# Softmax denominators of a graph attention layer: from matmuls in the aggregation to running sums over the sorted edges in the projection

## The reference

```python
xp = (x @ W).reshape(N, H, C)
e = leaky_relu(a_src[src] + a_dst[dst], 0.2)      # edges and one loop per node
m = segment_max(e, dst)
ee = exp(e - m[dst])
z = segment_sum(ee, dst)                          # the denominators
alpha = ee / z[dst]
out = segment_sum(xp[src] * alpha[:, :, None], dst)
x = x + relu(out + bias)
```

## Time and profile before

| what | value |
|---|---|
| median of the three runs | 1515.13 us (1513.52 to 1517.62) |
| profiled execution | 1526.42 us, span 1524.7 us |
| projection begins, by the first weights of line 1555 on the timeline | about 140 us |
| aggregation, from the end of the projection | about 519 to 1212 us |
| finish | about 1212 to 1524.7 us |

### The profile page before, as it was taken

One profiled execution on the slowest core, in us unless ns is written; L12 is line 12 of the kernel. 1 busy time (PEld: TensorE's weight loads), 2 busy tenths in 40 slices (PEclk: granted clock), 3 DMA queues, 4 the chain that ended last, 5 costly groups with the idle time before them and its releaser, 6 DMA issues. The chain is left out here.

```text
span 1524.7 us, 29568 instructions
## 1 busy us (share of the span) xinstructions
PE 1327.2 (87%) x10150; PEld 902.0 (59%) x10150; DVE 1081.6 (71%) x2255; ACT 1006.7 (66%) x2253; POOL 672.7 (44%) x610
## 2 busy tenths in 40 slices
PE   7998577899997678889899988888998769999997
PEld 5775244554443367777677777776777634544543
DVE  7997489889833567666676666676676787777771
ACT  3667478885445467777777777776777665666652
POOL 1003411111255466666666566665666244443441
PEclk9999799999998899999999999999999979999999
DMA  6784475543463698988898998988888857767752
GB/s 233 275 297 134 138 251 184 181 157 119 152 215 111 235 317 313 317 310 299 305 309 307 309 349 303 316 301 292 306 309 300 306 162 189 195 173 195 188 141 48
DMA packets 110549, 363.62 MB, mean 238 GB/s; under 512 B 20204, under 2 KB 20988, under 8 KB 110148
## 3 DMA queue, kind: packets, MB, share of 16 engines
q0 software_dynamic: 66048, 225.15, 45.7%
q1 hardware_dynamic: 40996, 135.71, 26.0%
q10 hardware_dynamic: 3360, 0.91, 0.2%
HBM read 299.78 MB, written 72.85 MB: 244 GB/s over the span
## 5 line engine op out<-in xcount | busy, mean ns | idle before, releaser
L1783 PE MATMUL sum_ps<-xg,wgt 128*128 128x256 f16 x4992 | 602.5, 277 | 91.5 <-issue 66.8
L1757 ACT ACTIVATE wgt<-hot,tables 128x128 f16<-128x128 f16 x1664 | 503.0, 388 | 187.8 <-PE sum_ps L1783 61.5
L1783 PEld LDWEIGHTS sum_ps<-xg,wgt 128*128 128x128 f16 x4992 | 475.5, 99 | 185.3 <-issue 112.8
L1682 POOL DMA_INDIRECT xg<-d_xp,tables x404 | 414.1, 1025 | 243.9 <-issue 98.3
L1555 PE MATMUL xp_ps<-acc 128*128 128x512 f16 x1152 | 274.3, 387 | 21.7 <-issue 11.9
L1741 DVE TENSOR_TENSOR acc<-sum_ps,acc 128x1024 f32 x220 | 268.1, 1219 | 1.4 <-issue 1.3
L2180 PE MATMUL fmm_ps<-xg,tables 128*128 128x512 f16 x1200 | 265.0, 381 | 4.0 <-DVE tables L2009 4.0
L2180 PEld LDWEIGHTS fmm_ps<-xg,tables 128*128 128x128 f16 x1200 | 117.8, 98 | 141.8 <-issue 7.1
L1555 PEld LDWEIGHTS xp_ps<-acc 128*128 128x128 f16 x1152 | 108.9, 99 | 146.6 <-issue 28.5
L1740 DVE TENSOR_TENSOR zsum<-z_ps,zsum 128x8 f32 x220 | 35.5, 162 | 217.1 <-PE z_ps L1793 75.4
L1712 DVE TENSOR_TENSOR wgt<-hot,tables 128x512 f16<-128x512 f16 x416 | 157.8, 418 | 0.0
(11 more groups left out here) (320 smaller groups left out, 1526.4 us busy)
## 6 DMA issues: line engine op xcount, KB each, us to landing
d_xnT<-acc SPq DMA_DIRECT2D x25, 512.0 KB, 3.6
tables<-d_lo SPq DMA_DIRECT2D x40, 320.0 KB
own_row<-d_own SPq DMA_DIRECT2D x25, 512.0 KB
wdT<-in_x_dram SPq DMA_DIRECT2D x24, 512.0 KB, 5.1
acc<-d_xnT SPq DMA_DIRECT2D x24, 512.0 KB
d_xp<-acc SPq DMA_DIRECT2D x24, 512.0 KB
d_own<-acc SPq DMA_DIRECT2D x24, 512.0 KB
xr<-in_x_dram SPq DMA_DIRECT2D x24, 512.0 KB
```

Source lines behind the costliest of these rows:

```text
L1682: nc.gpsimd.indirect_dma_start(out=xg[s][u][:, :, :].rearrange("p a n -> p (a n)"), out_offset=None, in_=d_xp, in_offset=bass.IndirectOffs ...
L1757: last = nc.scalar.activation(wgt[k % WB][:, u, h, :], hot[k % TURN][:, u, :], ACT.Copy, scale=col(numT[:, h, :], u, q))
L1783: last = nc.tensor.matmul(sum_ps[s][:, h * C:(h + 1) * C], w[:, u, a * HEADS + h, :], x[u][:, b, h * C:(h + 1) * C], start=(u == 0 and h % ...
```

## The change

VectorE forms in `project` a running sum of the edges' exponentials within each destination, with the scans that the maxima have: four scans over the lines at tile 19 (`line_sums`), the line ends transposed by TensorE and joined by a small scan at tile 20 (`sum_carries`), turned back by TensorE behind tile 22, and four scans with the carried start at tile 23 (`segment_sums`). SP stores the 784 KB to `d_segsum` at tile 24, and the wait for this store stands behind all others of the stage. In `aggregate` POOL gathers, behind the row gathers of steps 12 to 36, for each of the 25 node tiles the sum at the node's last edge. The denominator matmuls, their two PSUM buffers, the adds and their semaphore are gone; `mm_done` is raised by the last matmul of each half. `finish` takes the gathered sums, zeroed for nodes without edges.

```diff
@@ project
+        joined = sb("joined", [HEADS, 2, P])
+        line_sum = sb("line_sum", [HEADS, 2, P])
+        zcinT = sb("zcinT", [P, HEADS])
...
+                if t == BUSY + 13:
+                    sp.wait_ge(sums_ready, 1)
+                    sp.dma_start(g["d_segsum"].rearrange("(p c) h -> p (c h)", c=EC),
+                                 segmax[:, :, :].rearrange("p c h -> p (c h)")).then_inc(segmax_out, 16)
...
             for j in range(2):
                 sp.wait_ge(xp_out[j], 32 * (len(range(j, TILES, 2)) + (1 if j == LAST % 2 else 0)))
+            sp.wait_ge(segmax_out, 32)
...
-                nc.vector.memset(same[:, 0:1], 0.0)
+                nc.vector.memset(same[:, 0:1], 1.0)
...
+                nc.vector.tensor_copy(joined[:, 0, :], joins)
+                own.link(nc.vector.tensor_tensor(out=joined[:, 1, :], in0=whole, in1=joins, op=ALU.mult))
...
+            def running_sums(start):
+                for h in range(HEADS):
+                    last = nc.vector.tensor_tensor_scan(segmax[:, :, h], same[:, :], edge[:, :, h], start(h), ALU.mult, ALU.add)
+                return last
+
+            def line_sums():
+                dve.wait_ge(num_ready, 1)
+                dve.wait_ge(steps_read, 1)
+                running_sums(lambda h: 0.0).then_inc(ends_ready, 1)
+
+            def sum_carries():
+                dve.wait_ge(sums_turned, 1)
+                own.link(nc.vector.tensor_copy(line_sum[:, 0, :], gat_ps[1][0:HEADS, 0:P]))
+                own.link(nc.vector.tensor_tensor_scan(line_sum[:, 1, :], joined[:, 1, :], line_sum[:, 0, :], 0.0, ALU.mult, ALU.add))
+                nc.vector.memset(line_sum[:, 0, 0:1], 0.0)
+                nc.vector.tensor_tensor(out=line_sum[:, 0, 1:P], in0=line_sum[:, 1, 0:P - 1], in1=joined[:, 0, 1:P],
+                                        op=ALU.mult).then_inc(cin_ready, 1)
+
+            def segment_sums():
+                dve.wait_ge(cinT_done, 2)
+                dve.wait_ge(sums_turned, 1)
+                own.link(nc.vector.tensor_copy(zcinT[:, :], g_ps[:, 0:HEADS]))
+                running_sums(lambda h: zcinT[:, h:h + 1]).then_inc(sums_ready, 1)
...
+                if t == BUSY + 8:
+                    line_sums()
+                if t == BUSY + 9:
+                    sum_carries()
                 xp_rest(t - 1)
...
                 if t == BUSY + 12:
                     num_pairs()
                     own_logits()
+                    segment_sums()
...
+                if t == BUSY + 8:
+                    pe.wait_ge(steps_read, 1)
+                    pe.wait_ge(ends_ready, 2)
+                    nc.tensor.transpose(gat_ps[1][0:HEADS, 0:P], segmax[:, EC - 1, :], ident[:, :]).then_inc(sums_turned, 1)
+                if t == BUSY + 11:
+                    pe.wait_ge(cin_ready, 2)
+                    pe.wait_ge(wd_low, KC)
+                    nc.tensor.transpose(g_ps[:, 0:HEADS], line_sum[:, 0, :], ident[0:HEADS, 0:HEADS]).then_inc(cinT_done, 1)
                 if t in (BUSY + 9, BUSY + 10):
                     half = t - BUSY - 9
+                    pe.wait_ge(cin_ready, 2)
@@ aggregate
+        ZFROM = 2 * XB
...
             for k in range(XB, STEPS):
                 gather(k)
+                if ZFROM <= k < ZFROM + TILES:
+                    t = k - ZFROM
+                    nc.gpsimd.indirect_dma_start(
+                        out=zsum[:, t, :], out_offset=None, in_=g["d_segsum"],
+                        in_offset=bass.IndirectOffsetOnAxis(ap=g["last_i"][:, t:t + 1], axis=0)).then_inc(g["z_in"], 16)
...
-            nc.vector.memset(zsum[:, :, :], 0.0)
...
-                dve.wait_ge(z_added, k + 2)
...
-                nc.vector.tensor_tensor(out=z_acc, in0=z_ps[k % 2][:, 0:V], in1=z_acc, op=ALU.add).then_inc(z_added, 1)
...
-                    if u == 0:
-                        last.then_inc(mm_done, 1)
-
-                pe.wait_ge(z_added, k + 1)
-                for u in range(n):
-                    last = nc.tensor.matmul(z_ps[z][:, 0:V], hot[k % TURN][:, u, :], numT16[:, u * KT + q, :, 0],
-                                            start=(u == 0), stop=(u == n - 1))
-                last.then_inc(mm_done, 1)
+                    last.then_inc(mm_done, SUB // n)
@@ finish
-            own.link(nc.vector.tensor_tensor(out=z32[:, :, :], in0=zsum[:, :, 0:HEADS], in1=zsum[:, :, HEADS:2 * HEADS], op=ALU.add))
-            own.link(nc.vector.scalar_tensor_tensor(out=z32[:, :, :], in0=z32[:, :, :], scalar=1.0 / NUM_SCALE,
-                                                    in1=self_num[:, :, :], op0=ALU.mult, op1=ALU.add))
+            own.link(nc.vector.tensor_scalar(has01[:, :], g["has"][:, :], 0.0, None, ALU.is_equal))
+            dve.wait_ge(g["z_in"], 16 * TILES)
+            own.link(nc.vector.tensor_tensor(out=z32[:, :, :], in0=zsum[:, :, :],
+                                             in1=has01[:, :].unsqueeze(2).to_broadcast([P, TILES, HEADS]), op=ALU.mult))
+            own.link(nc.vector.tensor_tensor(out=z32[:, :, :], in0=z32[:, :, :], in1=self_num[:, :, :], op=ALU.add))
```

More of the change, by code:

```diff
@@ L161, in program @@
     d_segmax = nc.dram_tensor("d_segmax", (EP, HEADS), F32, kind="Internal").ap()
+    d_segsum = nc.dram_tensor("d_segsum", (EP, HEADS), F32, kind="Internal").ap()
     d_head = nc.dram_tensor("d_head", (EP, 2 * HEADS), F32, kind="Internal").ap()
@@ L201, in program @@
         first_idx = sb("first_idx", [P, SUB, XB], I32)
+        last_i = sb("last_i", [P, TILES], I32)
+        has = sb("has", [P, TILES])
         iota16 = sb("iota16", [P, P], F16)
@@ L219, in program @@
             w_scale_x = sb("w_scale_x", [P, 1])
-            has = sb("has", [P, TILES])
             start_i = sb("start_i", [P, TILES], I32)
-            last_i = sb("last_i", [P, TILES], I32)
             ntile128 = sb("ntile128", [P, KCOLS // P])
@@ L243, in program @@
                 sb, ps, sem = maker(back)
-                zsum = sb("zsum", [P, TILES, 2 * HEADS])
+                zsum = sb("zsum", [P, TILES, HEADS])
+                z_in = sem("z_in")
                 xg = [[sb(f"xg{j}_{u}", [P, 2, D], F16) for u in range(SUB)] for j in range(XB)]
@@ L946, in project @@
         nself_ready = sem("nself_ready")
+        sums_turned = sem("sums_turned")
+        sums_ready = sem("sums_ready")
         dve_own = sem("dve_own2")
@@ L1636, in aggregate @@
         sum_ps = [ps(f"sum_ps{j}", [P, D]) for j in range(SB)]
-        z_ps = [ps(f"z_ps{j}", [P, 512]) for j in range(2)]
         cleared = sem("cleared")
@@ L1646, in aggregate @@
         added = sem("added")
-        z_added = sem("z_added")
         block = ctx.enter_context(nc.Block())
         BEHIND = range(18, TILES - 1)
+        ZFROM = 2 * XB
         assert LEAD == XB and LEAD < KC
@@ L1736, in turn @@
                 dve.wait_ge(added, k + SB)
-                dve.wait_ge(z_added, k + 2)
                 s_acc = acc[:, bass.ds(t, 1), :].rearrange("p o n -> p (o n)")
-                z_acc = zsum[:, bass.ds(t, 1), :].rearrange("p o n -> p (o n)")
-                nc.vector.tensor_tensor(out=z_acc, in0=z_ps[k % 2][:, 0:V], in1=z_acc, op=ALU.add).then_inc(z_added, 1)
                 nc.vector.tensor_tensor(out=s_acc, in0=sum_ps[k % SB][:, :], in1=s_acc, op=ALU.add).then_inc(added, 1)
@@ L1768, in _ @@
             pe.sem_inc(added, SB)
-            pe.sem_inc(z_added, 2)
             def step(k):
                 q, n = PLAN[k]
-                s, z, x, w = k % SB, k % 2, xg[k % XB], wgt[k % WB]
+                s, x, w = k % SB, xg[k % XB], wgt[k % WB]
                 pe.wait_ge(arrived[k % XB], landed(k))
@@ L1818, in finish @@
         z32 = sb("z32", [P, TILES, HEADS])
+        has01 = sb("has01", [P, TILES])
         inv_z = sb("inv_z", [P, TILES, HEADS])
```

## The result

| kernel | median (runs) | profiled execution | span |
|---|---|---|---|
| before | 1514.33 us (4: 1513.13 to 1517.62) | 1526.42 us | 1524.7 us |
| after | 1543.73 us (4: 1542.14 to 1545.49) | 1542.96 us | 1541.4 us |

The change makes the kernel slower: ratio 1.0191, 95% interval [1.017, 1.0212], +29.4 us by the medians. Forecast was 1518 with a range to 1534; the time lies above the range. The two profiled executions differ by 16.5 us only, since that of before lies 12 us above its median. 1526.42 us lies within what one of these chips gave for the kernel before (1525.04 to 1530.98), and outside the four runs in the table. Which chip took them isn't recorded.

What follows compares the result with a forecast made beforehand. TensorE's aggregation steps were taken as the bound, with POOL's issue time on the path through TensorE's halts. Terms -22 - 8 + 32 + 1 + 0.1 gave +3 us, so 1518 us, range 1495 to 1534.

Steps and rivals of the forecast that it cites:

- the first case: Whole kernel: small gathers cost full POOL time against savings on TensorE; around 1518 us, 1510 to 1526, chance 0.52.
- the third case: Aggregation: POOL becomes the bound, so a faster TensorE only waits; +23 us, 1538, range 1527 to 1540, chance 0.18.
- Term (1): Aggregation: denominator matmuls leave TensorE, saving 0.11 us in each of 196 steps; -22 us, ends -16 and -27.
- Term (2): Aggregation: TensorE's instruction stream is 7.7% shorter, so its halts shrink as much; -8 us, ends 0 and -9.
- The argument against the third case: Aggregation: POOL still pauses 133 us for TensorE, and a TensorE quicker after each halt shortens those pauses.
- Term (3): Aggregation: VectorE loses 220 small adds, 35.5 us, but waits for TensorE before nearly each; counted as nothing.
- Term (4): Aggregation, steps 12 to 36: 25 small gathers cost their full POOL time; +32 us, ends +16 and 36.
- Term (5): Projection: running-sum scans, two transposes and the 784 KB store; scans 0, transposes +0.4, store +0.5, sum +1 us.
- Term (6): Start of the finish: one operation of 0.27 us added to the chain, less one that goes; +0.1 us.
- The reading of the halts: Aggregation: TensorE's instruction fetch doesn't finish during POOL's back-to-back indirect DMAs; TensorE waits until POOL's ring is full; 112.8 us.
- The second case: Aggregation: POOL's pauses half hide the small gathers, a shorter stream gains nothing; about 1507 us, 1488 to 1510, chance 0.30.
- The base: Whole kernel: +3 us set against the profiled 1526.4 us, its 11 us over the 1515.1 median carried over, giving 1518.

Runs made afterwards that it cites:

- no_small_gathers_third: The changed kernel without its 25 small gathers, sums set to zero, on a chip with halts: 1523.11 us against 1527.54 before, ratio 0.9962.
- no_small_gathers: The changed kernel without its 25 small gathers, sums set to zero, on a chip without halts: 1375.55 us, ratio 0.9947 to the kernel before.
- gathers_spread: The changed kernel with one small gather behind every eighth step from step 12 on, with halts: 1544.32 us, ratio 1.0187 to the kernel before.
- memsets_last_again: The changed kernel, small gathers replaced by POOL clearings, 14 in steps 12 to 25, 11 behind the last row gather; with halts: 1537.39 us, ratio 1.0064 to before.
- sums_only: The kernel before plus the projection's running sums, transposes and 784 KB store, nothing removed or gathered, without halts: 1384.53 us, ratio 1.0009.

## Why the prediction was wrong

The forecast was the first case, and the time came out a little above the third case's (1538, up to 1540; measured 1543.7). The third case's +23 is 6 short of +29.4: the parts that save gave 4 to 6 us net where it had 9 (by no_small_gathers_third), and by the two ratios, 1.0191 and 0.9962 on another chip, the small gathers cost 2.3%, 35 us or 1.4 us each, near the upper end of 36.

- **Term (1), -22 us, failed** in its size, by the pace of TensorE without the small matmuls. The step was: "the saving is 0.08 to 0.14; I take the middle, 0.11, over 196 steps". Taken as the distance between first weight loads, the steps from 40 on with two halves and no gap within them have a median of 2.67 us before and 2.62 after in the traces of the result. 79 of 107 after are at 2.62, 24 x 0.109. Another 20 are at 2.54, and there only the first two loads stand closer, 0.03 us apart. The same 0.109 was in the earlier trace rows: 20.88 us for 96 matmuls of 512 columns is 0.109 for each 256. The prediction took a tail off, had 2.59 for it, and then took the middle between that and the 2.53 which the loads filled beside the small matmuls. Measured is 0.05 a step, 10 us in 196 steps. Over all the steps with two halves from 40 on, halts included, the mean falls by 0.049 us in the traces of the result (3.226 to 3.177), by 0.024 to that of no_small_gathers_third (3.202), and by 0.036 without halts (2.713 to 2.677 in no_small_gathers); times 196 that is 10, 5 and 7 us.
- **Term (2), -8 us, failed** in its mechanism: 7.7% fewer instructions gave no less halting (112.7 us against 112.8, with the reserve above). What term (1) and (2) gave together is 9.1 us on a chip without halts, and on one with halts the 8.6 us in POOL's account. The third case had "-10" from POOL's pauses for it.
- **The argument against the third case failed**: that POOL's pauses are slack. The runs show they aren't. The third case came nearest, but in part by luck: it lets a faster TensorE wait for POOL at 2.65 us a step, and behind the small gathers no trace shows such a wait setting the step. TensorE is at 2.62 by itself, and POOL, at 2.61, just has nothing left to take up a small gather with. gathers_spread puts one issue into every eighth step, beside over 120 us of pauses, and pays for each. This is how I read it, from the earlier trace rows and memsets_last_again together: TensorE runs beside a burst for a while, 70 loads in the timeline above, but once it halts, it stands until POOL stops issuing, and POOL stops only when its ring is full. Any transfer added lengthens the burst, and TensorE stands still for it; and a TensorE that is faster between halts only comes to the next one sooner. This reading is argued. What the runs show is the price: a busy share of 62% and pauses of a third of a microsecond per gather told nothing of slack.
- **Term (3) held**, as far as seen: VectorE waits 159.0 us for TensorE ahead of its large adds. **Term (4) held** in size: +30.6 by itself without halts, and 31 us in steps 12 to 36 with them (105.5 against 74.3 in no_small_gathers_third, on another such chip). Forecast was 32.
- **Term (5) held**: sums_only is +2 with 0 to 3 forecast. **Term (6) held**: the finish is within 1 us.
- **The reading of the halts held** as to what prolongs them: POOL's issue of transfers, not its load. Two things in it weren't known: that it is a matter of the chip, and that it makes every issue on POOL cost, even where nothing waits for it. The Trainium skill (Runtime: NRT & Kernel Launch, Instruction fetch mechanics) calls the crossing of an instruction block "mostly hidden". If the halts are such crossings, the waits ahead of the weight loads agree on two of the chips here (1.1 to 2.5 us) and not on the others (99.8 to 129.3 us).
- **The second case**, gathers half hidden, is refuted on either kind of chip.
- **The base**: that the profiled execution's 11 us over the median were carried over did no harm; +29.4 against +3 is the error.

Only argued and not shown: why the halts come when they do, why two chips have none, and whether the fetch of instructions is what POOL's issues hold up. The profile names no releaser for them.

## What to carry to other kernels

An engine's pauses are slack only if nobody works in them: before an operation goes to an engine at 62%, add up its issue time per step (duration and the 0.3 us between two) and compare it with the pace of the bound; within a few per cent, the engine has nothing left, and what is added to it costs its full time. Price the removal of small operations from an unbroken run of the large ones (0.109 us a load), and not by the time that the small ones fill: of 0.14 us a step, 0.05 came back. An indirect gather took 1.24 to 1.33 us of POOL here with the 0.3 behind it, whether it brings 2 KB or 512 KB, so 25 gathers of 2 KB (31 us) outweighed 416 small matmuls with their adds (9 us). And lay the operations that you move to an "idle" stretch end to end against the engine that ends the stage.

## What the runs showed of the hardware

- The same kernel takes 1382 us on two chips and 1514 and 1528 us on two others. The finish is the same (315.4 and 315.9 us); the aggregation takes 574.3 against 684.6 us, and it begins 36 us sooner. In the aggregation what differs is TensorE's idle time of the kind "issue" ahead of the weight loads, 2.2 against 112.8 us.
- On the chips with halts, 11 indirect issues in a row slow TensorE to 27 weight loads in 15 us, with nothing that depends on them; 11 clearings of the same length don't.
- 256-column half-precision matmuls, each with its own weight load, follow one another every 0.109 us, 1022 in a row; two 8-column ones between them add 0.05 us and not the 0.14 that their loads fill.
- A stretch with long halts costs twice: the granted clock was 0.69 there and 0.84 over steps 12 to 36, against 1.00 without.
